# A decoder layer on one core: two stages of the last batch moved in the vector engine's order

## What is computed

```python
x = x + attn(layernorm(x), Wqkv, Wout)                  # 16 heads of 16, rotary, causal softmax
x = x + xattn(ctx_512, layernorm(x), Wq, Wk, gamma_raw) # (1-g)*layernorm(x) + g*A_learned
x = x + ffn(layernorm(x), gate_w, bias, w_gate, ...)    # 64 experts, 6 per token, and a shared one
```

## Time and profile before

| | us |
|---|---|
| median of 3 runs | 301.0 |
| lowest and highest run | 300.43, 301.64 |
| span of the profiled execution | 299.4 |
| VectorE busy | 207.2 (69%) |
| TensorE busy | 226.2 (76%) |
| GpSimd busy | 134.1 (45%) |
| ScalarE busy | 95.6 (32%) |

### The profile page before, as it was taken

How to read it: one execution, slowest core, us unless ns; L and a number is a source line. 1 busy time by engine, 2 the same in 40 slices (tenths; PEclk the granted TensorE clock), 3 DMA queues, 4 the chain that set the end, 5 groups by cost and what they waited for, 6 DMA issues and landing times.

```text
span 299.4 us, 5226 instructions
## 1 busy us (share of the span) xinstructions
PE 226.2 (76%) x1836; PEld 165.8 (55%) x1836; DVE 207.2 (69%) x668; ACT 95.6 (32%) x154; POOL 134.1 (45%) x182
## 2 busy tenths in 40 slices
PE   8883586598889888879566214494989999896993
PEld 3672475486678577659335103243457766653882
DVE  3699999979989998987692671912145334751697
ACT  1444530522434555566154014010013333333000
POOL 2810767616115300236677757777204655673000
PEclk9999589599999999999978755588699999999899
DMA  6608979694085999923208999990599999921996
GB/s 213 195 0 108 106 110 168 95 124 87 0 107 78 305 398 382 350 72 134 93 27 259 283 283 298 300 244 14 107 200 211 255 262 217 279 83 41 378 387 198
DMA packets 36890, 55.78 MB, mean 186 GB/s; under 512 B 6556, under 2 KB 26790, under 8 KB 36864
## 3 DMA queue, kind: packets, MB, share of 16 engines
q1 hardware_dynamic: 31680, 47.75, 62.6%
q10 hardware_dynamic: 768, 3.54, 5.7%
q0 software_dynamic: 4416, 4.15, 4.8%
HBM read 32.93 MB, written 25.17 MB: 194 GB/s over the span
## 4 chain that ended last, share of the span: by engine, by line
POOL 18%; PE 15%; issue 11%; DVE 10%; DMA 6%; another core or an unknown queue 4%; ACT 2%; ACTq 0%; POOLq 0%; SPq 0%; DVEq 0%
POOL slot_rows L996 15%; PE unit L644 5%; PE proj L663 3%; DMA arena<-expert_rows 2%; DVE arena L1432 2%; DMA arena<-slot_rows 2%; PE unit L630 2%; DVE arena L1168 2%; PE outp L653 1%; DVE arena L1434 1%; POOL rstd L897 1%; DVE arena L1438 1%; DMA slot_rows<-rows,arena 1%; DVE arena L1436 1%
## 5 line engine op out<-in xcount | busy, mean ns | idle before, releaser
L996 POOL DMA_INDIRECT slot_rows<-rows,arena x48 | 47.6, 992 | 23.9 <-issue 12.1
L1018 POOL DMA_INDIRECT expert_rows<-arena x28 | 28.3, 1010 | 34.0 <-ACT arena L870 27.5
L805 ACT ACTIVATE arena<-unit 128x1024 f32<-128x1024 f32 x24 | 24.6, 1024 | 42.8 <-PE unit L488 37.4
L1168 DVE TENSOR_REDUCE arena<-unit 128x4 f32<-128x1024 f32 (+1 forms) x24 | 28.9, 1212 | 3.1 <-PE unit L475 3.1
L1057 DVE MAX8 arena<-arena 128x8 f32<-128x256 f32 x80 | 30.6, 414 | 0.3
L488 PE MATMUL unit<-arena 128*128 128x256 bf16 (+1 forms) x128 | 29.2, 248 | 0.0
L1062 DVE MATCH_REPLACE8 arena<-arena 128x256 f32<-128x256 f32 x72 | 29.0, 409 | 0.0
L487 PE MATMUL unit<-arena,identb 128*128 128x128 bf16 x128 | 25.8, 222 | 0.0
L895 POOL TENSOR_SCALAR nmean<-mv 128x2 f32<-128x2 f32 x12 | 2.8, 236 | 46.0 <-DVE mv L1095 41.4
L486 PE MATMUL unit<-arena 96*128 96x128 bf16 (+1 forms) x96 | 22.3, 253 | 0.6 <-ACT arena L805 0.6
L475 PE MATMUL unit<-arena,identb 128*128 128x128 bf16 x128 | 20.8, 227 | 0.0
(11 more groups left out here) (221 smaller groups left out, 550.9 us busy)
## 6 DMA issues: line engine op xcount, KB each, us to landing
ring<-in_w_gu SPq DMA_DIRECT2D x16, 384.0 KB
expert_rows<-blank SPq DMA_DIRECT2D x8, 768.0 KB, 9.5
arena<-in_w_gu SPq DMA_DIRECT2D x16, 384.0 KB, 13.3
arena<-expert_rows SPq DMA_DIRECT2D x7, 768.0 KB, 9.2
slot_rows<-blank SPq DMA_DIRECT2D x1, 4608.0 KB, 17.3
arena<-slot_rows ACTq DMA_DIRECT2D x12, 288.0 KB
arena<-ring_dn SPq DMA_DIRECT2D x24, 128.0 KB, 4.5
ring_dn<-in_w_dn SPq DMA_DIRECT2D x16, 192.0 KB
```

The lines of the kernel that those rows point to most:

```text
L805: act_fn(prob[:, n, :], unit_at((key, b)), ACT.Exp, scale=D ** -0.5).then_inc(unit_free((key, b)), 1)
L996: pool.indirect_dma_start(out=slot_dram, out_offset=bass.IndirectOffsetOnAxis(ap=place[:, t, k:k + 1], axis=0), in_=rows[:, t, :], in_offs ...
L1018: pool.indirect_dma_start(out=z_dram, out_offset=bass.IndirectOffsetOnAxis(ap=rowi[:, p:p + 1], axis=0), in_=yrow[:, p % NY, :], in_offset ...
L1168: v.tensor_reduce(nmax[:, t, c * u:c * u + c], unit_at((key, b)).rearrange("p (h k) -> p h k", k=n), axis=AX, op=ALU.max, negate=True).the ...
```

## The change

Two entries of the list move, both of batch 3; nothing else is touched.

```diff
-    F1 Z3 U14 G2 U24 F3 D1e2 Z3 G16 U34 G5 F5 P1 U44 D22 U54 ME4 D1b3 G5 D1a3 Z1 D3a2 F1 D1c3 Z5 G5 D1d3 F2 Z4 F1 G2 D1e3
-    F1 Z2 F1 D3b2 G1 R2 Z1 G48 F1 D23 Z1 P2 Z5 D3a3 F1 D3b3 Z4 F1 R3 MS4 G1
+    F1 Z3 U14 G2 U24 F3 D1e2 Z3 G16 U34 G5 F5 P1 U44 D22 U54 ME4 D1b3 G5 F9 D1c3 D1a3 Z1 D3a2 F1 Z5 G5 D1d3 F2 Z4 F1 G2 D1e3
+    F1 Z2 F1 D3b2 G1 R2 Z1 G10 F1 D23 G38 Z1 P2 Z5 D3a3 F1 D3b3 Z4 F1 R3 MS4 G1
```

## The result

The changed kernel took 308.25 us (median of 4 runs, 305.85 to 311.83), the kernel before in the same comparison 301.32 us. The ratio is 1.0232, with a 95% interval of 1.0147 to 1.0317: slower, as forecast. The forecast time was 307.0 us. Now and then an execution of either kernel is slower as a whole, and here one of four was on each side (311.83 and 308.62 us); the ratio leaves such runs out, as all medians and ratios further down do, and without them the medians are 306.64 and 301.0 us.

The account below looks back on a forecast made before the run. GpSimd's queued placements were taken to set the expert phase's start. Wait, mixing and 38 steps put the 25th placement 6.0 us later: span 299.4 + 6.0 = 305.4, plus 1.6 outside it, 307.0 us; range 305.2 to 308.7.

Parts of the forecast that it names:

- The bound: GpSimd's 48 queued placements set the expert phase's start; no idle behind the 25th could take up a shift.
- Edit one: Vector engine, heads' division ahead of the adjacency's addition: 0.5 us loss alone, hidden by the other edit's wait.
- edit two: Vector engine, batch 3's mixing after 10 of 48 routing steps: 25th placement 5.5 to 6.5 us later.
- 2.7 us of cover: Batch 3's statistics, ending near 168.0 us, stay that far ahead of GpSimd's reading them at 170.66 us.
- step 1: Vector engine idle before the mixing, from about 170.0 to 174.15 us, waiting for ScalarE's L760.
- Step 2: Vector engine: the mixing and its statistics run 1.88 us, to 176.03 us.
- Step 3: Vector engine: the third pair's 38 remaining routing steps take 6.48 us, upper end 6.91, to 182.51 us.
- the shift of the 25th placement: GpSimd: start moves from 176.75 to 182.79 us, so 6.0 us later, between 5.5 and 6.5.
- A: Rival: the mixing finds its input ready and costs only 1.88 us: 302.9 us; chance 0.05.
- B: Rival: the weight transfers' drain, not the placements' end, starts the experts: down to 301.0 us; chance 0.03.
- C: Rival: TensorE returns to full clock later, first expert matmuls slower by 1.5 to 3 us: 308.6 to 310; chance 0.06.

Follow-up runs that it names:

- mixing_alone: The kernel before with only batch 3's mixing moved from behind the 48th to behind the tenth routing step: 306.9 us, ratio 1.0263.
- mix_after_28: The kernel before with batch 3's mixing behind the 28th routing step instead of the 48th: ratio 1.0086.
- both_last: The changed kernel, unedited, run once more beside a run of the kernel before: ratio 1.0157 to before.
- routing_early: The kernel before with batch 2's router logits ahead of batch 3's projection and 28 third-pair routing steps ahead of the projection's addition: ratio 1.0025.
- routing_early_22: As routing_early, but with 22 instead of 28 routing steps ahead of the addition of batch 3's projection: ratio 1.0003.
- before_profiled: The kernel before, unchanged, run for a second profile of it: median 299.8 us, span 297.0 us.

## Why the prediction was right

**The bound.** Right. The 25th placement's start moved, and the end with it; from there to the expert phase nothing gave time back (41.20 us before, 40.2 to 41.6 us after).

**Edit one costs nothing here and half a microsecond alone.** Right: 0.45 us at L574 and 0.37 us at the gap alone, none on top of edit two (11.50 against 11.51 us). Its time alone was 1.0 us above before, more than that, and the rest is not explained. One sentence was too sure, too: the 2.7 us of cover for batch 3's statistics hold only while TensorE is on time. In the changed kernel's first profile, where its transposes of the heads were 2.3 us late and the clock was 0.55 from 157 to 165 us, the statistics came 1.82 us too late. In mixing_alone the clock was as low but the transposes had come in time, and 1.0 us of cover was left (169.43 to 170.46 us).

**Edit two, step 1, the wait.** Right: L1209 at 174.29 us where 174.15 was forecast, released by L760 as named. Step 2: the mixing and its statistics take 1.80 us up to the next routing step (174.29 to 176.09), forecast 1.88.

**Step 3, the 38 steps.** This term was mis-sized. Forecast 6.48 us, upper end 6.91; measured 5.91 us (176.09 to 182.00, L1320's end), and the same 5.90 in the first profile. The direction of the reasoning was right (with GpSimd idle beside them the steps take less time), but the fourth pair's steps, which I took as the clean case, were lengthened while GpSimd worked as well: their L1284 took 0.51 us and not 0.23, and their L1257 0.35 us and not 0.17. That is why the gap is 5.4 us wider instead of 6.0. It is 5.65 us wider than in the second profile of before, where the same 38 steps took 6.57 us (169.45 to 176.02) and not 6.91.

**The time.** 307.0 us forecast, 308.25 measured with 305.85 to 311.83 about it, or 306.64 without the slowest. The close hit is partly luck: the shift of the 25th placement was 0.4 to 0.6 us smaller than forecast, and what other parts of the program lose in some executions, in which TensorE's clock was lower, made up for it. In the four comparisons the difference was between 5.0 and 8.5 us, so it is the gap that bears the sum out, and not the time.

**The rivals.** A (the input is there, only 1.9 us) is what mix_after_28 shows, behind step 28 and not behind step 10. B (the drain of the weights starts the experts) didn't occur: the first expert transposes moved with the 25th placement in every profile. C (the clock around the experts) is real as a spread of 4.6 us in the expert phase between executions of the changed kernel, 80.2 to 84.8 us. The wait doesn't have to bring it, for both_last had the wait and 0.98; whether it makes it likelier is open, as said above.

## What to carry to other kernels

Before work that waits is pulled forward in an in-order queue, find the moment at which its input comes and who sets it; here that was another engine's queue of ten placements. Everything behind the pulled work waited with it: 38 short steps, the last of which releases the 25th placement. A step whose successor stands behind a full queue gains nothing from being earlier. And when the idle in one place is closed, look at once where the next late arrival stands: with the routing ahead of the addition it moved from the 25th placement to the norm.

## What the hardware showed that was not expected

A vector-engine instruction can run on, or stand still, until one of GpSimd's indirect DMAs ends; such delays are seen not only beside GpSimd's arithmetic. In the kernel before, in the fourth pair's routing:

```profile
187.66 0.97 POOL L996 DMA_INDIRECT slot_rows<-rows,arena  x1 [0.30 <-issue]
188.27 0.35 DVE L1257 COPY arena<-arena 128x8 f32<-128x8 f32 x1
...
190.21 0.97 POOL L996 DMA_INDIRECT slot_rows<-rows,arena  x1 [0.31 <-issue]
190.72 0.51 DVE L1284 TENSOR_SCALAR arena<-arena 128x128 bf16<-128x128 f32 x1
```

L1284 takes 0.23 us where GpSimd is idle (179.02 us in both_last); here it ends at 191.23 us, 0.05 us behind the end of the placement that was running. L1257 takes 0.17 us in the changed kernel and 0.35 here, and ends at 188.62 us with the placement beside it (188.63). In the third pair's routing it did the same: 0.34 us, to 170.59 us, the end of the 23rd placement. Both lengthenings come back in the fourth pair's routing of both_last (L1257 to 194.14 us, the placement to 194.13; L1284 to 196.74, the placement to 196.69). In routing_early L1284 waited 1.64 us and started at 168.83 us:

```profile
167.72 0.97 POOL L996 DMA_INDIRECT slot_rows<-rows,arena  x1 [0.30 <-issue]
...
168.83 0.23 DVE L1284 TENSOR_SCALAR arena<-arena 128x128 bf16<-128x128 f32 x1 [1.64 <-remote]
```

That is 0.14 us behind the end of a placement. In routing_early_22 L1284 waited 2.21 us, through the end of a placement (170.40 us) and GpSimd's small operations, and started at 172.19 us, just behind the end of one of these, L899 at 172.18 us:

```profile
171.88 0.30 POOL L899 TENSOR_SCALAR rstd<-rstd,gam 128x2 f32<-128x2 f32 x1
```

The Trainium skill, "SBUF — State Buffer", section "Who interferes with whom", says that the shared pair of ports is an exclusive lock and that tensor_scalar is among the vector operations that can take it. These starts agree with that as far as they go. The same instruction had no such wait in the changed kernel, where GpSimd stood idle. But it isn't so at every placement: L1284 took its 0.23 us beside one in the kernel before (173.48 us, the placement from 173.46 to 174.54) and in the fourth pair's routing of before_profiled (190.27 us, the placement from 189.76 to 190.74). Why it hits L1284 in one order and L1264 or L1267 in another, and why in routing_early it passed over one gap between placements (167.41 to 167.72 us), the rows don't show, and no run took the cause apart.
